# Four graph layers on one core: eight biases move from TensorE to GpSimd, norms' intermediates stay in PSUM, order planned anew

## The reference

```
layer 0: q,k = x@W+b; v = x@W; 12 heads of 32; scores + beta*adj, masked where adj is 0; softmax; @ v
layer 1: twice: u = h (h W_left/right^T)^T / sqrt(384), left above the diagonal, right below
                att = exp(u)*adj / sum;  h = relu(norm(att @ (h W_lin^T + b_lin)))
layer 2: twice: a = softmax(h h^T / sqrt(384)) * adj / sum
                ctx = upper(a) @ (h Wl^T + bl) + diag(a) * (h Ws^T + bs) + lower(a) @ (h Wr^T + br)
                h = relu(norm(ctx))
layer 3: attention with Wq, Wk, Wv (+ bv), then Wo (+ bo)
```

## Time and profile before

| | |
|---|---|
| median of 3 runs | 2934.89 us (2932.13 to 2945.61) |
| the profiled execution | 2933.42 us |
| its span, first to last instruction | 2931.7 us |
| PE busy | 2823.5 us, 96% |
| DVE busy | 2403.6 us, 82% |
| ACT busy | 1825.3 us, 62% |
| POOL busy | 1349.7 us, 46% |
| granted TensorE clock, mean | 0.988 |

### The profile page before, as it was taken

How to read it: one execution, slowest core, us unless ns; L and a number is a source line. 1 busy time by engine, 2 the same in 40 slices (tenths; PEclk the granted TensorE clock), 3 DMA queues, 4 the chain that set the end, 5 groups by cost and what they waited for, 6 DMA issues and landing times.

```text
span 2931.7 us, 93395 instructions
## 1 busy us (share of the span) xinstructions
PE 2823.5 (96%) x35008; PEld 2091.8 (71%) x35008; DVE 2403.6 (82%) x8566; ACT 1825.3 (62%) x4885; POOL 1349.7 (46%) x2571
## 2 busy tenths in 40 slices
PE   6899999999999999999999999999999999999996
PEld 4666767777777777777777777777777777777764
DVE  6867888788888888888888888888888878888767
ACT  5745566566666666666666666666666666665546
POOL 2334454354454454454454454454454445444545
PEclk9899999999999999999999999999999999999997
DMA  9414354344444444444454454444443444544325
GB/s 238 86 30 72 67 101 77 61 84 70 84 86 68 84 85 72 83 86 69 84 84 71 84 84 71 85 84 70 85 84 70 82 77 80 91 79 75 56 39 101
DMA packets 803991, 237.41 MB, mean 81 GB/s; under 512 B 771544, under 2 KB 803416, under 8 KB 803424
## 3 DMA queue, kind: packets, MB, share of 16 engines
q1 hardware_dynamic: 795808, 218.28, 42.3%
q10 hardware_dynamic: 7744, 13.17, 1.4%
HBM read 29.99 MB, written 12.58 MB: 15 GB/s over the span
## 4 chain that ended last, share of the span: by engine, by line
PE 76%; DMA 7%; DVE 6%; ACT 3%; POOL 3%; SPq 2%; issue 2%; ACTq 0%; DVEq 0%; POOLq 0%
PE bank L801 10%; PE bank L802 9%; PE bank L803 9%; PE bank L789 8%; PE bank L790 7%; PE bank L791 7%; PE bank L893 6%; DMA turned<-flat 6%; PE bank L838 4%; PE bank L807 3%; PE bank L886 2%; PE bank L823 2%; PE bank L825 2%; PE bank L824 2%; DVE score L974 2%
## 5 line engine op out<-in xcount | busy, mean ns | idle before, releaser
L789 PE MATMUL bank<-turned,w_hi 128*128 128x128 f16 x4608 | 817.2, 220 | 19.7 <-DMA turned<-flat 17.7
L790 PE MATMUL bank<-turned,w_hi 128*128 128x128 f16 x4608 | 816.4, 220 | 0.0
L791 PE MATMUL bank<-turned,w_lo 128*128 128x128 f16 x4608 | 816.3, 220 | 0.0
L801 PE MATMUL bank<-w_hi,turned 128*128 128x384 f16 x2112 | 692.4, 328 | 23.7 <-DVE w_lo L925 14.2
L802 PE MATMUL bank<-w_lo,turned 128*128 128x384 f16 x2112 | 691.0, 327 | 0.0
L803 PE MATMUL bank<-w_hi,turned 128*128 128x384 f16 x2112 | 690.8, 327 | 0.0
L716 ACT ACTIVATE score<-score,small 128x128 f32<-128x128 f32 x1536 | 500.9, 391 | 152.7 <-DVE small L980 138.0
L707 ACT ACTIVATE ab<-bank 128x384 f16<-128x384 f32 (+1 forms) x768 | 367.0, 484 | 254.3 <-PE bank L791 130.8
L609 POOL TENSOR_TENSOR flat<-score,flat 128x384 f16<-128x384 f32 x256 | 237.2, 927 | 613.6 <-ACT flat L722 613.0
L789 PEld LDWEIGHTS bank<-turned,w_hi 128*128 128x128 f16 x4608 | 453.8, 98 | 51.8 <-DMA turned<-flat 22.4
L790 PEld LDWEIGHTS bank<-turned,w_hi 128*128 128x128 f16 x4608 | 453.9, 99 | 18.6 <-issue 13.1
(11 more groups left out here) (116 smaller groups left out, 6559.0 us busy)
## 6 DMA issues: line engine op xcount, KB each, us to landing
turned<-flat SPq DMA_TRANSPOSE x960, 2.8
x<-x_dram SPq DMA_DIRECT2D x64, 192.0 KB, 2.4
out_dram<-score SPq DMA_DIRECT2D x64, 192.0 KB, 2.2
w_stage<-w_dram ACTq DMA_DIRECT2D x19, 576.0 KB, 5.6
adj<-adj_dram SPq DMA_DIRECT2D x64, 64.0 KB, 2.3
rows<-rows_dram ACTq DMA_DIRECT2D x1, 1920.0 KB, 9.3
turned<-bias_dram SPq DMA_DIRECT2D x4, 9.0 KB
beta<-beta_dram SPq DMA_DIRECT2D x1, 0.5 KB, 6.3
```

The source lines that it names most:

```text
L789: pe.matmul(dst, lhsT=w_hi[:, w, k, cols], rhs=t_hi[u][:, k, :], start=(k == 0), stop=False)
L790: pe.matmul(dst, lhsT=w_hi[:, w, k, cols], rhs=t_lo[u][:, k, :], start=False, stop=False)
L791: last = pe.matmul(dst, lhsT=w_lo[:, w, k, cols], rhs=t_hi[u][:, k, :], start=False, stop=(k == DT - 1 and w not in BIAS_OF))
L801: pe.matmul(dst, lhsT=t_hi[u][:, k, :], rhs=w_hi[:, w, k, :], start=(k == 0), stop=False)
```

## The change

- Weights 5, 8 and 9 to 14 have no bias matmul any more. A new part of POOL, `("bias", w)`, adds the bias row to the projection in SBUF behind ACT's copy, and `mix` waits for it.
- `rows` grows from 10 to 18 rows and is loaded in two parts, behind the sixth and the fourteenth weight.
- The `e` tiles and the inner norm's intermediates stay in the bank in which their matmul left them: `zc` and `z` of `inner` and `gain`, `e` of both kinds. Banks are freed later (`READ_BY`).
- Two 128x1 copies of DVE (L1044, L1082) fall away; `denominator` takes two instructions in place of four.
- The weights' stages lie in the SBUF tiles of the seventh unit, so this unit is loaded only when the last weight is split; `bias_rows` holds 3 biases in place of 11.
- `PERIOD`, `SHIFTED` and all wanted times and durations of `PARTS` are new, and so are the orders and banks.

```
-BIAS_OF = {L0_Q: 0, L0_K: 1, 5: 2, 8: 3, 9: 4, 10: 5, 11: 6, 12: 7, 13: 8, 14: 9, L3_V: 10}
-NB = 3
-NR = 10
+BIAS_OF = {L0_Q: 0, L0_K: 1, L3_V: 2}
+NB = 1
+ROW_OF = {5: 6, 8: 7, **{w: 3 + w for w in range(9, 15)}}
+NR = 18
-PERIOD = 43.452
+PERIOD = 42.394
...
-    (PE, "project", 9): (499.73, 1.629, 1.809, ((SYNC, "turn", 3),), ()),
+    (PE, "project", 9): (484.06, 1.464, 1.644, ((SYNC, "turn", 3),), ()),
+    (POOL, "bias", 9): (391.94, 0.920, 1.050, ((SCALAR, "project", 9),), ()),
-    (PE, "mix", 2): (502.90, 2.010, 2.240, ((VECTOR, "turn_delta", 0), (SCALAR, "project", 9), (SCALAR, "project", 10), (SCALAR, "project", 11)), ()),
+    (PE, "mix", 2): (458.24, 2.010, 2.240, ((VECTOR, "turn_delta", 0), (POOL, "bias", 9), (POOL, "bias", 10), (POOL, "bias", 11)), ()),
...
-ROWS_AFTER = 6
+ROWS_AFTER, ROWS_SPLIT = (5, 13), 8
-           "turn_adj": lambda k: (SCALAR, "turn_adj", k), "u_gcn": lambda k: (VECTOR, "u_gcn", k),
-           "u_di": lambda k: (SCALAR, "u_di", k), "turn_delta": lambda k: (VECTOR, "turn_delta", k),
-           "mix": lambda k: (VECTOR, "inner", k)}
+           "turn_adj": lambda k: (SCALAR, "turn_adj", k), "u_gcn": lambda k: (VECTOR, "delta_gcn", k),
+           "u_di": lambda k: (VECTOR, "delta_di", k), "turn_delta": lambda k: (VECTOR, "turn_delta", k),
+           "mix": lambda k: ((VECTOR, "turn", 2), (VECTOR, "residual", 1), (VECTOR, "turn", 4), (VECTOR, "residual", 2))[k]}
...
+    comes_after(((SYNC, "load", 0), UNITS - 1), ((VECTOR, "weight", WEIGHT_ORDER[-1]), 0))
...
-        w_stage = [sb(f"w_stage_{slot}", [128, DT * D])[:, :] for slot in range(STAGES)]
+        w_stage = [last_unit[:, n * DT * D:(n + 1) * DT * D] for n in range(STAGES)]
+        def e_of(i, name, layer):
+            return bank(name, layer, i)[:, 0:N]
+        def inner_of(i, k):
+            return bank("mix", k, i)[:, 0:D]
...
@block.sync
             def load(i, k):
+                if i == UNITS - 1:
+                    sp.wait_ge(w_lo_made, NW)
@block.gpsimd
+            def bias(i, w):
+                u = i % UNITS
+                pool.wait_ge(*proj_hi_done.at(i, "made", w))
...
+                made = proj[u][2 if w < 9 else (w - 9) % 3]
+                pool.tensor_tensor(made, made, rows[:, ROW_OF[w], :], ALU.add).then_inc(biased.of(i), 1)
...
-                step("part of sum", DENOM, col(u, ZSUM), constant(DEN_EPS), ALU.mult)
-                step("sum", DENOM, col(u, DENOM), col(u, DSUM), ALU.add)
-                step("sum squared", DENOM, col(u, DENOM), col(u, DENOM), ALU.mult)
-                pool.tensor_tensor(col(u, EPS), col(u, DENOM), constant(INNER_EPS), ALU.mult).then_inc(gpsimd_done.of(i), 1)
+                pool.tensor_scalar(col(u, DENOM), col(u, ZSUM), 1e-10, col(u, DSUM), ALU.mult, ALU.add).then_inc(gpsimd_done.of(i), 1)
+                pool.wait_ge(*gpsimd_done.at(i, "sum", layer))
+                pool.tensor_scalar(col(u, EPS), col(u, DENOM), col(u, DENOM), 1e-12, ALU.mult, ALU.mult).then_inc(gpsimd_done.of(i), 1)
@block.scalar
-                act.activation(e[u], e[u], ACT.Exp).then_inc(scalar_done.of(i), 1)
+                act.activation(e_of(i, "u_gcn", layer), e_of(i, "u_gcn", layer), ACT.Exp).then_inc(scalar_done.of(i), 1)
@block.tensor
-                    pe.wait_ge(*proj_hi_done.at(i, "made", L1_W[k][2]))
+                    pe.wait_ge(*biased.at(i, "made", L1_W[k][2]))
...
-                        pe.wait_ge(*proj_hi_done.at(i, "made", w))
+                        pe.wait_ge(*biased.at(i, "made", w))
@block.vector
-                dve.tensor_tensor(e[u], u_pair[u][:, 0, :], u_pair[u][:, 1, :], ALU.add).then_inc(mixed_out.of(i), 1)
+                dve.tensor_tensor(e_of(i, "u_gcn", layer), u_pair[u][:, 0, :], u_pair[u][:, 1, :], ALU.add).then_inc(mixed_out.of(i), 1)
-                dve.scalar_tensor_tensor(zc[u], made[:, 0:D], mv[u][:, 0:1], rows[:, 2 * k, :], ALU.subtract, ALU.mult)\
+                dve.scalar_tensor_tensor(inner_of(i, k), made[:, 0:D], mv[u][:, 0:1], rows[:, GAIN_ROW[k], :], ALU.subtract, ALU.mult)\
-                dve.scalar_tensor_tensor(z[u], zc[u], col(u, GAIN if k < 2 else ROOT), rows[:, 2 * k + 1, :], ALU.mult, ALU.add)\
+                dve.scalar_tensor_tensor(inner_of(i, k), inner_of(i, k), col(u, GAIN if k < 2 else ROOT), rows[:, GAIN_ROW[k] + 1, :], ALU.mult, ALU.add)\
-                    dve.scalar_tensor_tensor(z[u], z[u], 0.0, x[u], ALU.max, ALU.add).then_inc(mixed_out.of(i), 1)
+                    dve.scalar_tensor_tensor(z[u], inner_of(i, 2 * layer - 1), 0.0, x[u], ALU.max, ALU.add).then_inc(mixed_out.of(i), 1)
-                dve.tensor_copy(col(u, TICK), constant(HALF))
```

More of the change, by code:

```diff
@@ L52 @@
[L52 to L57, removed]
@@ L65 @@
[L65 to L70, removed]
@@ L233 @@
-    (SYNC, "turn", 5): (933.49, 1.240, 3.150, ((POOL, "turn", 5),), ()),
+    (PE, "mix", 1): (0.00, 0.700, 0.830, ((POOL, "bias", 8), (VECTOR, "delta_gcn", 1)), ()),
+    (POOL, "inner", 1): (38.86, 0.515, 0.635, ((VECTOR, "inner", 1),), ()),
+    (PE, "turn_adj", 0): (77.82, 0.120, 0.380, ((VECTOR, "scores", 3),), ()),
+    (POOL, "turn", 0): (86.70, 0.868, 0.964, ((SCALAR, "turn", 0),), ()),
+    (VECTOR, "scores", 3): (157.22, 0.629, 0.353, ((PE, "scores", 3), (VECTOR, "scores_lo", 2)), ()),
@@ new lines @@
+    (POOL, "bias_x", 0): (208.82, 0.961, 1.093, ((POOL, "turn", 0),), ()),
+    (VECTOR, "project", 1): (209.48, 0.442, 0.590, ((SCALAR, "project", 1),), ()),
+    (VECTOR, "gain", 1): (211.52, 0.916, 1.088, ((POOL, "inner", 1),), ()),
+    (SYNC, "turn", 0): (230.29, 1.240, 2.888, ((POOL, "turn", 0),), ()),
+    (VECTOR, "scores_lo", 2): (239.63, 0.441, 0.600, ((SCALAR, "scores", 2),), ()),
+    (POOL, "turn", 3): (246.15, 0.870, 0.966, ((SCALAR, "turn", 3),), ()),
+    (VECTOR, "masks", 0): (254.64, 0.516, 0.668, ((SYNC, "load", 0),), ()),
@@ new lines @@
+    (SCALAR, "turn", 4): (281.37, 0.412, 0.580, ((VECTOR, "gain", 2),), ()),
+    (SCALAR, "project", 13): (283.23, 0.387, 0.553, ((PE, "project", 13),), ()),
+    (POOL, "bias", 11): (283.27, 0.920, 1.050, ((SCALAR, "project", 11),), ()),
+    (SYNC, "turn", 6): (284.39, 1.240, 2.888, ((POOL, "turn", 6),), ()),
+    (SCALAR, "scores", 3): (284.43, 1.493, 1.673, ((VECTOR, "scores", 3), (SYNC, "scores", 2)), ()),
+    (SCALAR, "attend", 0): (285.14, 0.133, 0.308, ((PE, "attend", 0),), ()),
+    (VECTOR, "gain", 3): (285.98, 0.525, 0.677, ((POOL, "inner", 3),), ()),
@@ new lines @@
+    (POOL, "residual", 0): (338.27, 1.134, 1.285, ((VECTOR, "residual", 0),), ()),
+    (SCALAR, "project", 6): (340.17, 0.370, 0.536, ((PE, "project", 6),), ()),
+    (PE, "scores", 2): (341.67, 0.360, 0.540, ((SCALAR, "scores", 1),), ()),
+    (PE, "mix", 0): (344.17, 0.700, 0.830, ((POOL, "bias", 5), (VECTOR, "delta_gcn", 0)), ()),
+    (PE, "attend", 1): (344.73, 0.234, 0.454, ((SYNC, "scores", 1),), ()),
+    (SCALAR, "turn", 1): (345.49, 0.413, 0.581, ((SCALAR, "norm", 0),), ()),
+    (POOL, "turn", 5): (345.58, 0.867, 0.963, ((SCALAR, "turn", 5),), ()),
@@ L502, in graph_layers @@
         low_made = signal("low_made", POOL, {"turn": ("x",), "bias_x": ("biased",), "scores": ("p",)})
+        biased = signal("biased", POOL, {"bias": ("made",)})
         gpsimd_done = signal("gpsimd_done", POOL, lambda name, k: {
             "turn_adj": ("upper", "lower"), "minus_adj": ("minus",),
-            "sums": ("part of sum", "sum", "sum squared", "constant"),
+            "sums": ("sum", "constant"),
             "inner": ("inner root",) if k < 2 else ("variance", "inner root"),
```

456 lines of the change are left out of this document (232 added, 224 removed).

## The result

The changed kernel takes **3005.5 us** (median of 4 runs, 3003.6 to 3006.8) against 2936.7 us for the kernel before (4 runs): ratio **1.023**, 95% interval 1.021 to 1.0247. The forecast was 2864 us, with a range of 2834 to 2896. The change made the kernel slower by 69 us, outside the range.

A forecast was written before the change was run, and what follows sets the result against it. PE's instruction list was taken to bound the middle; -73.1 - 2.7 + 3 + 5 + 2 - 5 = -70.8 us from 2933.4 gave 2862.6, and 1.5 us for the median of runs made 2864 us, range 2834 to 2896.

The forecast's parts named there:

- Cost 0 in the middle: Middle: the roughly 1 us latency from projection to mix costs nothing, as PE has other units' matmuls among seven in flight.
- New order: Middle: replanned lists change PE's idle time of 35 us; taken as -5 us, between -30 and +15.
- What bounds it: Middle: PE works through a list at 44.34 us a unit, nobody holds it up, only a shorter list helps.
- Matmuls, -76: PE: eight of nine bias matmuls go at 0.1625 us each: -73.1 us in the middle, -2.7 from 150 to 300 us.
- Adds, 0: POOL: 512 bias adds near 1.04 us, 8.29 us a unit, POOL 66% busy and no bound; cost 0 in the middle.
- PSUM, 0: DVE: intermediates in PSUM bring DVE from 37.2 to 35.2-36.4 us a unit; PE doesn't wait for DVE, so time 0.
- Banks, +3: Middle: mix and u banks held longer, 16 to perhaps 30 of 344 bank-us a unit: +3 us, between 0 and +11.
- Start, +5: First 150 us: the seventh unit is loaded late and rows take more DMA time: +5 us, between 0 and +17.
- end, +2: End: the last units' four mixes wait for a 1.04 us add instead of a 0.16 us matmul: +2, at most +3.5.
- POOL blocks DVE: Rival, 3%: eight adds a unit block DVE instructions with two SBUF inputs, 46.1 us a unit: 3030 us, slower.
- The adds show: Rival, 11%: PE waits one late add of 1.04 us in each of 56 units, +58 us: 2922 us.
- The signs: Expected profile: period 42.8 to 43.2 us, DVE down 60 to 130 us; wrong if PE's middle idle exceeds 60 us.

The follow-up runs named there:

- b_no8: Kernel before, order and banks kept, the eight bias matmuls left out and their biases not added: 2873.5 us against 2932.3 beside it.
- a_noadds: Changed kernel, order and banks kept, POOL's 512 bias adds left out and the eight biases not added: 2950.0 us.
- a_new0: Changed kernel with the same instructions and an order searched anew (wanted times, PERIOD, SHIFTED, trace durations, margin): 2886.6 us, 0.981 of the kernel before.
- b_p435: Kernel before with PERIOD 43.5 in place of 43.452 and nothing else changed: 2981.4 us, ratio 1.017.
- a_margin: Changed kernel with only the durations in PARTS replaced by trace durations and 0.22 us of margin: 2992.6 us, ratio 1.020.
- a_oldwants: Changed kernel with the wanted times of the kernel before in PARTS, durations, PERIOD and SHIFTED as changed: 3166.8 us, ratio 1.080.
- a_sbuf: Changed kernel, order and banks kept, the e tiles and the inner norm's intermediates back in SBUF: 3046.2 us, ratio 1.037.

## Why the prediction was wrong

**The step that failed** is the cover and the order: "Cost 0 in the middle", because "with seven units in flight PE has other units' matmuls to do, and the order is made with that wait in it", and the term "New order", -5 us with +15 as its worst. PE does not choose among seven units on the chip; it has one list. I had written that no engine picks its work and still reckoned as if a late result were covered by whatever else is ready. The new order was taken at -5, yet with the same matmuls and no adds, b_no8 and a_noadds are 77 us apart, and with the same instructions altogether the changed kernel and a_new0 119. The adds were taken at nothing and cost 51 to 55 us in this order.

What makes this order bad is known in part. It was planned with adds of 0.92 us, nothing late and nobody kept out of SBUF. But the plan of the kernel before did the same, and its order holds. The measured difference between the two lists is that one repeats from unit to unit and the other does not: the three orders of complete kernels that don't repeat (b_p435, a_margin and the change's own) all take 2981 us or more, and of the six that do, five take 2943 us or less. The sixth, a_oldwants, shows that it isn't enough. No run changes the repetition of the change's order and nothing else, so as a cause it is a strong suspicion.

The runs account for the 69 us, each beside its own runs of the kernel before: -59 for the matmuls in the old order (b_no8), +77 for order, late seventh unit and PSUM together, of which PSUM is a gain (a_sbuf), +51 for the adds in this order (a_noadds).

**Point by point.**
- *What bounds it.* Right: PE's list did, and taking 83 us off it gave 59 at once.
- *Matmuls, -76.* The count was right; the size was 59 in the old order. The -2.7 for 150 to 300 us is not what failed: at 43.23 us a unit b_no8 already misses a third of the 1.30 in the even stretch.
- *Adds, 0.* Mis-sized: 51 to 55 us in the order of the change, 13 to 17 in a fitted one. The length of an add was right.
- *PSUM, 0.* The direction on DVE was right, the price wrong: 41 us. I put DVE's savings at nothing since PE doesn't wait for DVE's total. In a fixed list PE waits for single DVE results, and there a stretch from 0.62 to 1.4 us can count, though DVE's share of the span is 80% with PSUM and 81% without.
- *Banks, +3.* Not tried apart. Among PE's waits in the middle, the DVE passes that now free the mix banks (L997, L1120) end 1 us; the readers of the banks of scores and attention (L1019, L765) end some 19, against 3 for the same readers before.
- *New order, -5.* This term and the adds are what failed. I had reckoned that a worse order could lose as much as a better one could win, PE's idle time of 35 us, and took +15 as its worst; one constant of the planner loses 49 (b_p435).
- *Start, +5, and end, +2.* The first 150 us lost 0.19 unit, 8 us, and the next 150 us won most of it back. The end lost about 9.
- *Rivals.* "POOL blocks DVE" had the sign and a true mechanism, but the wrong way for it to act: I let it decide only when DVE is 95% busy. DVE's busy time fell; the adds cost it 89 us in all, 1.4 of the 8.3 us a unit that I feared, and the exclusion cost by when it struck. "The adds show", +58, is near the 51 to 55 of a_noadds by luck: PE was to wait for one add a unit, and in the profile it never waits for POOL. That a new order could lose 77 us and more was no rival at all, though the change gave every part a new wanted time.
- *The signs.* L807 (L842 now) has its 64 instructions, the new line is near 1.04 us and L1109's mean is next to its median. DVE was to fall by 60 to 130 us and fell by 12: the copies and the scale-and-shift gave their 52 us each, but DVE's low halves (L985, L1030 now) grew by 26 us and the divisions by 37. PE's idle time in the middle passed the 60 us that I had set as a sign of being wrong (139), but neither the adds nor the readers of the mix banks are what ended it.

## What to carry to other kernels

Where a planner fixes every engine's list, the order is part of the kernel and has to be fitted anew with each edit. The searches that did it here took durations from a trace and put lateness in; how much each of these gives isn't shown. A cheap thing to look at first is whether the lists still repeat from unit to unit. A new order deserves its own term, as large as the spread of orders (49 us for one constant here), and its own run with the instructions unchanged. Busy shares say what a stretch can cost at best; what a late result costs is decided by what stands behind it in the lists. To see whether work that was moved to another engine is bad or only badly placed, take it out once in the given order and once in a fitted one: some 53 and 15 us here.

## What was not expected of the hardware

- DVE instructions with two SBUF inputs wait for POOL instructions that read SBUF far more than for ones that write: L1055 has a median of 0.30 us and took 1.12 beside an add; the mean of L1030 is 668 ns beside adds, 609 beside fills of the same length, 588 without either. With one input in PSUM (L1109) none of 220 took longer than 627 ns in the changed kernel, and the mean was 622 to 623 ns beside adds, beside fills and without either.
- DVE instructions that read and write the same PSUM bank are hardly slower: L1109 reads and writes the bank with a median of 625 ns, and from and to SBUF it is 619.
